# Attention scores of 32 sequences: four groups of 32 rows instead of two of 64, and the keys' two parts written from PSUM by two engines

## The reference

```python
x = x + L0_xattn(_layernorm(x), ctx, ...)      # 16 heads of 16, softmax(Q K^T * 0.25) V
x = x + L0_ffn(_layernorm(x), ...)             # one of 8 experts for each token, by argmax
x = x + L1_xattn(_layernorm(x), ctx, ...)      # 8 heads of 32, / 16, then q + attn, layer norms, Wo, relu
x = x + L1_ffn(_layernorm(x), ...)             # two of 8 experts for each token
```

## Time and profile before

| | |
|---|---|
| median of 3 runs | 2231.89 us (2225.58 to 2285.02) |
| the profiled execution's own time | 2223.33 us |
| its span | 2221.6 us |
| mean granted clock of TensorE | 0.933 |
| busy: PE, PEld | 1721.6 us (77%), 1272.6 us (57%) |
| busy: DVE, ACT, POOL | 1030.7 us (46%), 896.1 us (40%), 1033.6 us (47%) |

### The profile page before, as it was taken

How to read it: one execution, slowest core, us unless ns; L and a number is a source line. 1 busy time by engine, 2 the same in 40 slices (tenths; PEclk the granted TensorE clock), 3 DMA queues, 4 the chain that set the end, 5 groups by cost and what they waited for, 6 DMA issues and landing times. The chain is left out here.

```text
span 2221.6 us, 45766 instructions
## 1 busy us (share of the span) xinstructions
PE 1721.6 (77%) x14350; PEld 1272.6 (57%) x14351; DVE 1030.7 (46%) x2291; ACT 896.1 (40%) x1823; POOL 1033.6 (47%) x1421
## 2 busy tenths in 40 slices
PE   5888888888864999958777777777775268888884
PEld 4666666666643666646666565656664135555552
DVE  3555555555534222224555555554455724444442
ACT  3666666666641222225444444444442011111110
POOL 4656666666631111134544555454543036666663
PEclk8999999999986999978989999999997589999998
DMA  4111111000014111120111111100000222222223
GB/s 111 41 46 59 44 63 44 26 26 19 20 31 163 33 33 33 33 73 12 51 40 61 47 48 41 48 23 27 25 23 12 94 80 36 38 38 38 38 38 81
DMA packets 54163, 102.08 MB, mean 46 GB/s; under 512 B 11842, under 2 KB 37674, under 8 KB 50698
## 3 DMA queue, kind: packets, MB, share of 16 engines
q1 hardware_dynamic: 37754, 78.87, 11.0%
q0 software_dynamic: 16352, 22.47, 5.5%
HBM read 79.78 MB, written 24.93 MB: 47 GB/s over the span
## 5 line engine op out<-in xcount | busy, mean ns | idle before, releaser
L950 DVE TENSOR_REDUCE a_mx<-a_SM 100x2 bf16<-100x722 f32 x384 | 350.2, 912 | 351.1 <-PE a_SM L423 349.2
L1533 PE MATMUL e_PH<-w,e_xT 128*128 x712 | 326.5, 602 | 6.0 <-DVE e_ab L1665 2.9
L695 ACT ACTIVATE a_Pr<-a_ST 120x800 f32<-120x800 f32 (+1 forms) x288 | 241.8, 854 | 46.6 <-PE a_ST L459 46.4
L423 PE MATMUL a_SM<-a_KTb,a_QMb 64*100 64x361 bf16 x768 | 136.9, 353 | 133.2 <-DVE a_mx L950 131.0
L745 POOL TENSOR_TENSOR a_rstd<-a_ve,a_powers 100x1 f32<-100x1 f32 x192 | 117.4, 611 | 223.2 <-DVE a_ve L919 223.1
L1533 PEld LDWEIGHTS e_PH<-w,e_xT 128*128 128x128 f32 x712 | 134.8, 193 | 141.4 <-issue 138.6
L1454 POOL COPY e_gidx<-toks 128x1 int32 (+1 forms) x89 | 48.6, 546 | 300.2 <-PE e_PX L1522 206.7
L470 PE MATMUL a_M<-a_Pr,a_V 120*32 120x100 f32 (+3 forms) x4608 | 186.6, 262 | 0.3 <-ACT a_Pr L695 0.3
L423 PEld LDWEIGHTS a_SM<-a_KTb,a_QMb 64*100 64x100 bf16 x768 | 47.0, 119 | 225.8 <-DVE a_mx L950 187.1
L1619 ACT ACTIVATE e_hT<-e_PT 128x512 f32<-128x512 f32 x57 | 34.0, 597 | 332.7 <-PE e_PY L1556 309.2
L452 PE MATMUL a_ST<-a_MXM,a_ones_bf 64*120 64x400 bf16 (+1 forms) x576 | 104.1, 357 | 68.3 <-POOL a_MXM L833 67.1
(11 more groups left out here) (194 smaller groups left out, 4038.2 us busy)
## 6 DMA issues: line engine op xcount, KB each, us to landing
w<-in_E_w SPq DMA_DIRECT2D x24, 1024.0 KB, 5.9
a_ct<-in_ctx SPq DMA_DIRECT2D x64, 362.0 KB, 3.2
keep_rows<-a_keep SPq DMA_DIRECT2D x64, 100.0 KB
tile_rows<-e_y SPq DMA_DIRECT2D x32, 128.0 KB
b_rows<-in_E_b SPq DMA_DIRECT2D x1, 4096.0 KB
sums<-X SPq DMA_DIRECT2D x1, 3200.0 KB
out<-sums SPq DMA_DIRECT2D x2, 1600.0 KB, 9.4
X<-in_x SPq DMA_DIRECT2D x1, 2800.0 KB
```

What stands on the lines that cost most here:

```text
L423: last = nc.tensor.matmul(SM[0:LQ, half, 0:LK], QMb[rows, chunk, m, :], KTb[rows, chunk, :], start=True, stop=True)
L695: nc.scalar.activation(dst.rearrange("p (j q) -> p j q", j=2), ST[0:n, (b.p * NS + s) % 2, :, 0:4 * LQ], ACT.Exp, scale=SCALE).then_inc(ex ...
L950: V_.tensor_reduce(pair, SM[0:LQ, :, 0:LK], AX_X, ALU.max).then_inc(max_done, 1)
L1533: last = nc.tensor.matmul(PH[:, h, :], xT[:, c, :], rhs, start=(c == 0), stop=(c == DC - 1))
```

## The change

A product of the scores now takes 32 partitions, four groups side by side, and each group writes to a PSUM bank of its own: ST is one tile of four banks, all heads of one key tile, where it was two tiles of two. So there are 3 score blocks in both layers, each of 4 bf16 and 24 F32R products (of 200 columns in layer 0, of 100 in layer 1), and one exp of 1600 elements for each. `HT` becomes 2 and 1; layer 1 has no mask any more, `MXM` is `mxT` itself, `QM` is written by ACT and `QL` is `qf` - `QM`. `values` goes by key tile over all heads, between the score blocks. `score_rows` reads `QM` and `KT` in place of the bf16 copies, which are gone. ACT writes `KT` from PSUM (`copy_k`), DVE writes `KL` from PSUM (`low_keys`), and the latter now frees M1. `front` comes ahead of `max_columns`; `front_end` is part of `project`. In layer 1 the token-wise q is a transpose of `qf`, which holds the bias, so `bqb` is gone; on DVE `tail1a` and `tail1c` stand ahead of the maxima, on POOL `power(2, ...)` moves to the next step.

```diff
-TILE_ROWS = (64, 64)
+ROWS = 32
+GROUPS = 128 // ROWS
...
     HT = ROWS // HD
+    PER = DC * HT
...
+    NS = 3
...
-        e, j, t = pos // 8, pos % 8 // 4, pos % 4
-        if ROWS == 128:
-            return slice(0, 128), j, t
-        return slice(64 * j, 64 * j + 64), t // HT if layer == 1 else e, t % HT
+        r, t = pos // PER, pos % PER
+        return slice(ROWS * r, ROWS * r + ROWS), t // HT, t % HT
...
-        QMb = sb("QMb", [128, DC, HT, LQ], BF16)
-        KF = sb("KF", [128, DC, LK])
-        KT = [sb(f"KT{p}", [128, DC, LK], F32R) for p in range(2)]
-        KL = [sb(f"KL{p}", [128, DC, LK], F32R) for p in range(2)]
-        KTb = sb("KTb", [128, DC, LK], BF16)
+        KT = [sb(f"KT{p}", [128, DC, LKP], F32R) for p in range(2)]
+        KL = [sb(f"KL{p}", [128, DC, LKP], F32R) for p in range(2)]
...
-        MXM = sb("MXM", [128, DC, HT, LQ], BF16)
+        MXM = sb("MXM", [128, DC, HT, LQ], BF16) if layer == 0 else mxT[:].unsqueeze(2)
...
-        ST = ctx.enter_context(nc.psum_tensor(tag + "ST", [128, 2, 2, 512], F32))
+        ST = ctx.enter_context(nc.psum_tensor(tag + "ST", [128, GROUPS, 512], F32))
...
+            def project(b):
...
-            def front_end(b):
                 pe.wait_ge(qf_ready, b.count(1, 1))
                 last = project_v(b, 0, M0, 0)
                 if layer == 1:
                     for c in range(DC):
-                        last = nc.tensor.matmul(M0[0:LQ, D:2 * D], xT[:, c, :], wq[:, c, :],
-                                                start=(c == 0), stop=(c == DC - 1))
+                        last = nc.tensor.transpose(M0[0:LQ, D + c * 128:D + (c + 1) * 128], qf[:, c, :], ident[:])
...
                 if j == 0:
-                    pe.wait_ge(ktb_ready, b.count(2, 2))
-                    pe.wait_ge(qmb_ready, b.count(1, 1))
+                    pe.wait_ge(kt_ready, b.count(2, 2))
+                    pe.wait_ge(qm_ready, b.count(1, 1))
                 pe.wait_ge(max_done, b.count(NP, j))
                 for half in range(2):
-                    rows, chunk, m = place(j // 4 * 8 + half * 4 + j % 4)
-                    last = nc.tensor.matmul(SM[0:LQ, half, 0:LK], QMb[rows, chunk, m, :], KTb[rows, chunk, :],
+                    rows, chunk, m = place(half * NP + j)
+                    last = nc.tensor.matmul(SM[0:LQ, half, 0:LKP], QM[b.p][rows, chunk, m, :], KT[b.p][rows, chunk, :],
...
-                kt, eight = SLOTS[s]
-                k0, n = KTILES[kt]
-                buf = (b.p * NS + s) % 2
-                if kt == 0:
-                    pe.wait_ge(mxm_ready, b.count(EIGHTS, eight + 1))
-                    pe.wait_ge(ql_ready, b.count(EIGHTS, eight + 1))
+                k0, n = KTILES[s]
                 if s == 0:
-                    pe.wait_ge(kl_ready, b.count(1, 1))
+                    pe.wait_ge(mxm_ready, b.count(1, 1))
+                    pe.wait_ge(ql_ready, b.count(1, 1))
+                    pe.wait_ge(k_evac, b.count(2, 2))
                     if b.low >= 1:
                         pe.wait_ge(norm_read, b.count(1))
-                if b.low >= 1 or s >= 2:
-                    pe.wait_ge(exp_done, b.count(NS, s - 1))
-                C = DC // EIGHTS
-                for j in range(2):
-                    rows = place(8 * eight + 4 * j)[0]
-                    nc.tensor.matmul(ST[0:n, buf, j, 0:4 * LQ], ones_bf[rows, 0:n],
-                                     MXM[rows, C * eight:C * eight + C, :, :], start=True, stop=False)
+                if b.low >= 1 or s >= 1:
+                    pe.wait_ge(exp_done, b.count(NS, s))
+                for r in range(GROUPS):
+                    rows = place(PER * r)[0]
+                    nc.tensor.matmul(ST[0:n, r, 0:PER * LQ], ones_bf[rows, 0:n], MXM[rows, :, :, :],
+                                     start=True, stop=False)
 
                 for k, (K, Q) in enumerate(((KT[b.p], QM[b.p]), (KT[b.p], QL), (KL[b.p], QM[b.p]))):
-                    for t in range(0, 4, HT):
-                        for j in range(2):
-                            rows, chunk, _ = place(8 * eight + 4 * j + t)
-                            last = nc.tensor.matmul(ST[0:n, buf, j, t * LQ:(t + HT) * LQ], K[rows, chunk, k0:k0 + n],
-                                                    Q[rows, chunk, :, :], start=False, stop=(k == 2 and t + HT == 4))
+                    for t in range(0, PER, HT):
+                        for r in range(GROUPS):
+                            rows, chunk, _ = place(PER * r + t)
+                            last = nc.tensor.matmul(ST[0:n, r, t * LQ:(t + HT) * LQ], K[rows, chunk, k0:k0 + n],
+                                                    Q[rows, chunk, :, :], start=False, stop=(k == 2 and t + HT == PER))
                 last.then_inc(st_ps, 1)
 
-            def values(b, g, last_exps=False):
-                for kt in range(3):
-                    n = KTILES[kt][1]
-                    if last_exps and kt == 2:
-                        pe.wait_ge(exp_done, b.count(NS, NS))
+            def values(b, kt):
+                n = KTILES[kt][1]
+                pe.wait_ge(exp_done, b.count(NS, kt + 1))
+                for g in range(NG):
                     for j in range(HG):
                         h = g * HG + j
                         last = nc.tensor.matmul(M0[VW * j:VW * (j + 1), g * LQ:(g + 1) * LQ],
                                                 V[b.p][0:n, kt, h, :], Pr[0:n, kt, POS[h] * LQ:(POS[h] + 1) * LQ],
-                                                start=(kt == 0), stop=(kt == 2))
+                                                start=(kt == 0 and g == 0), stop=(kt == 2 and g == NG - 1))
...
             def step(b, fr, ahead, back, tail):
                 nxt, nxt2, prev = b.plus(1), b.plus(2), b.plus(-1)
+
+                def rows_of(*pairs):
+                    if fr:
+                        for j in pairs:
+                            score_rows(nxt, j)
+
+                if fr:
+                    front(nxt)
                 if back:
                     max_columns(b)
                 if fr:
-                    front(nxt)
+                    project(nxt)
                 if back:
                     scores(b, 0)
-                if fr:
-                    front_end(nxt)
-                pair = 0
-                for s in range(NS):
-                    if back:
-                        if s == 4:
-                            pe.wait_ge(exp_done, b.count(NS, 3))
-                            free_m0(nxt, fr)
-                            values(b, 0)
-                        if s > 0:
-                            scores(b, s)
+                rows_of(*((0, 1), (0,))[layer])
+                if back:
+                    scores(b, 1)
+                if tail:
                     if fr:
-                        score_rows(nxt, pair)
-                        pair += 1
-                    if tail and s == 2 + (1 - layer):
-                        if fr:
-                            pe.wait_ge(v_evac, nxt.count(2, 1))
-                        out_transposes(prev, layer == 1, prev.low >= LAG)
-                for g in range(EARLY, NG):
-                    if back:
-                        late = g == max(EARLY, EARLY_EXPS)
-                        if late:
-                            pe.wait_ge(exp_done, b.count(NS, NS - 1))
-                        if g == 0:
-                            free_m0(nxt, fr)
-                        last = values(b, g, late)
-                    if tail and g == 1:
-                        out_product(prev, layer == 1, prev.low >= LAG)
-                    if fr and layer == 0 and g == 2:
-                        score_rows(nxt, 6)
+                        pe.wait_ge(v_evac, nxt.count(2, 1))
+                    out_transposes(prev, layer == 1, prev.low >= LAG)
+                rows_of(*((2,), (1,))[layer])
                 if back:
-                    last.then_inc(av_ps, 1)
+                    free_m0(nxt, fr)
+                    values(b, 0)
+                rows_of(*((3,), ())[layer])
+                if back:
+                    scores(b, 2)
+                rows_of(*((), (2,))[layer])
+                if back:
+                    values(b, 1)
+                rows_of(*((4,), ())[layer])
+                if tail:
+                    out_product(prev, layer == 1, prev.low >= LAG)
+                rows_of(*((5,), ())[layer])
+                if back:
+                    values(b, 2).then_inc(av_ps, 1)
+                rows_of(*((6,), ())[layer])
                 if ahead:
                     start_k(nxt, nxt2, prev, tail)
-                if fr:
-                    score_rows(nxt, NP - 1)
+                rows_of(NP - 1)
...
             def copy_k(b, h):
 
-                act.wait_ge(kl_ready, b.count(1))
-                act.wait_ge(ktb_ready, b.count(2))
                 act.wait_ge(k_ps, b.count(2, h + 1))
```

(89 more changed lines are left out.)

99 lines of the change are left out of this document (35 added, 64 removed).

## The result

The changed kernel takes 2174.12 us (median of 4, 2173.72 to 2176.48) against 2258.0 us (median of 4, 2225.58 to 2285.02). The ratio is 0.9757, 95% interval 0.9731 to 0.9784; it is that of the undisturbed executions, hence nearer to 1 than the two medians. Run again (e12) the kernel had 0.9695, 0.9655 to 0.9736. So it is faster by 2.4 to 3%, where I had forecast 2140 us, 4.1% under the median of 2232 that I had. The profiled execution took 2174.32 us, 49.0 less than the one before; I had laid out 92.

A forecast was written before the change was run, and what follows sets the result against it. Layer 0 was taken as mostly TensorE's own work, layer 1 as a ring of waits. 2223.3 - 10 (layer 0) - 82 (layer 1) = 2131 us profiled, median 2140; own range 2095 to 2185, 8 in 10 from 2080 to 2235.

The forecast's parts named there:

- the last one of layer 1: Layer 1's TensorE waits: longest hole shrinks to 1.7 us, so the low clock, 0.68 us of the mean step, goes.
- Rival 3: Clock in both layers: each pays 0.68 us a step, + 42 us, median 2182; chance 0.12.
- Layer 1's step: Layer 1's attention stage: a step goes from 22.15 to 19.5 us, 82 us over 31 intervals.
- S0 to S1: Layer 1's first to second score block: starts at 7.0 and 9.85 us, the second waiting for the first exp.
- S1 to S2: Layer 1's second to third score block: starts at 9.85 and 12.8 us, with value products between.
- The POOL wait: Layer 1, before the scores: TensorE's 2.3 us wait for POOL's masked maximum goes.
- TensorE's wait for DVE ahead of the value products: Layer 1: q done at 2.75 us, the second `low_keys` ends at 4.4, value products start at 4.45.
- Layer 0's step: Layer 0's attention stage: a step goes from 19.34 to 19.0 us, 10 us over 31 intervals.
- the seven spacings of rows: Layer 0's eight row products: seven spacings of 1.36 us, bounded by DVE, 9.5 us whatever TensorE does.
- Rivals 1, 2 and 5: Four-group score rounds: two at a time, median 2239, chance 0.12; hindering each other, from 2278, 0.06; short rounds cheaper, 2103, 0.1.
- rival 5: Score rounds on TensorE: 100 columns cost 0.05 us, 200 cost 0.09; median 2103 us; chance 0.1.
- Rival 4: DVE becomes the ring, `low_keys` holding M1: 1.4 us more a step, + 87 us, median 2227; chance 0.1.

The follow-up runs named there:

- e12: The changed kernel, unedited, run once more against the kernel before: 2159.33 us.
- e1: The changed kernel with unread 128-row products put into TensorE's waits in both layers, against the kernel before: 2088.63 us, ratio 0.9367.
- e11: e1 run once more, against the kernel before: 2093.07 us, ratio 0.9399.
- e2: The changed kernel with the filling of e1 over 32 rows only, against the kernel before: 2120.44 us, ratio 0.9499.
- e5: The changed kernel with the filling of e1 over 64 rows, against the kernel before: 2112.67 us, ratio 0.9431.
- e9: The changed kernel with only the 8 filling products of e1 ahead of layer 1's value products, against the kernel before: 2132.91 us, ratio 0.96.
- e6: e1 with layer 1's second `low_keys` ahead of `tail1b` and 2 instead of 8 fillers before its value products, against the kernel before: 2139.15 us, ratio 0.9569.
- e4: The changed kernel with two groups of 64 rows in layer 0 alone, against the kernel before: 2199.35 us, ratio 0.9879.

## Why the prediction was wrong

The time lay inside the stated range and the direction was right, but the gain forecast, 92 us, came as 49. The step that failed is the last one of layer 1: "TensorE's longest hole, 2.25 us or more before, is then 1.7, so I take the low clock away as well".

- **The clock.** The longest hole did shrink, and the clock went down to 0.83 in place of up to 1.00. Layer 1 runs at 17.9 us a step at full clock, the mean of the loop's two steps, and took 20.64: 2.75 x 31 = 85 us. Layer 0 runs at 18.75 and took 19.16: 13 us. Rival 3 had the place right and the size wrong, 42 us for both, since it took the price of the kernel before. e1 and e11 show that the loss is the clock: the same kernel with its waits filled gets 86 and 66 us back. The change halves the score products' columns and rows and shortens the holes; I counted only the holes. What makes the clock fall is not settled: e2 and e5 rule out idle time alone, e9 the longest hole alone, and e6 beside e9 speaks against the plain sum of filling. Whether the fewer rows or the fewer columns of the score products lowered the clock was not tested apart. The Trainium skill, TensorE: Matmul & The Clock Gate, section Why this matters for your kernels, keeps the clock up by leaving no long idle gaps between bursts. That is not enough in this trace: behind layer 1's first step no wait of TensorE was over 1.75 us, it was busy for 554 of 640 us (83% of the two full-clock steps), and the clock was 0.83, while before it had waits of 2.25 us in every step, was busy 73% of the time, and had 0.94.
- **Layer 1's step** was laid out as 19.5 and is 17.9 at full clock: 50 us too slow. S0 to S1 is 1.84 us (1435.81 to 1437.65) where I had 2.85. Of that 1.0, 0.7 is the exp, laid out with 1600 elements and 1.55 us where layer 1 has 800 and 0.84; the other 0.3 is the block itself and its drain, laid out too long. S1 to S2 is 2.50 (1437.65 to 1440.15, right behind the value products) where I had 2.95. The POOL wait went as forecast; TensorE's wait for DVE ahead of the value products came where it was forecast, 1.16 us in this step and up to 1.73 in others, for 1.7 laid out.
- **Layer 0's step**, 19.0, is 18.75 (21 of its 31 steps ran at full clock, 18.7 to 18.9): 8 us too slow. The mechanism is half right. Of the seven spacings of rows one is 1.34 and four are 1.42 to 1.52, near the 1.36 that DVE's maximum sets, but two are 2.00 and 1.94, those with a score block between. With blocks 0.64 us longer (e4) the step grew by 1.65, so TensorE's own work bounds a part of it.
- **Together** 2131 - 50 - 8 + 85 + 13 + 3 = 2174. Two errors of opposite sign met, which is luck: with layer 1's and layer 0's steps laid out right, the clock would have been the whole miss, about 100 us. The median of 2140 has 8.6 us more, the distance of the earlier profiled execution from its median; the changed kernel's median and profiled execution lie 0.2 us apart.
- **Rivals 1, 2 and 5** are out: rounds take 0.105 us with four groups, for 200 and for 100 columns. The Trainium skill's rule beside rival 5 (TensorEngine Tiling (Array Packing), Theoretical Speedup) gives 64 rows up to two times and 32 up to four times the throughput, so at most 2 from one to the other: a block of layer 0 shrank by 1.76 (1.48 to 0.84, e4), near that rule, one of layer 1 from 0.93 at most (1312.54 to the value product at 1313.47) to 0.73 us, a factor of 1.3, far from it. That the load of 120 weights sets the short round fits both, but no run changed it alone.
- **Rival 4** is half there: `low_keys` holds TensorE in both layers, but at no more than its laid out price.

## What to carry to other kernels

Where a change takes work from TensorE or gives each of its products fewer rows, read the granted clock of that stage as a term of the sum, not only its waits: here it ate 98 us (85 + 13) of the 150 that the full-clock steps promise (0.6 and 4.25 us, x 31). A clock that was lost here could be bought back with products that nobody reads, placed in waits on a bank that is free there; how many rows they had counted, and the number of them alone did not tell what they would give. And a step that alternates between clocks has to be compared at its full-clock steps, and, in a loop of two, with its own counterpart, before its waits are argued over. Last, redo the element counts for every layer that a change touches: here an exp of 1600 elements was carried over to a layer that has 800, and the forecast was 0.7 us a step out by it.

## What the runs showed that was not expected

- Filling TensorE's waits with unread products shortened the kernel by 86 us (2174 to 2089; 66 us, 2159 to 2093, the second time), with 980 more products in the two stages (14 a step in layer 0, 18 in layer 1).
- Layer 1's clock was 0.98 filled with 128 rows, 0.95 with 64, 0.93 with 32, though TensorE idled for 22, 13 and 18 us there; unfilled it was 0.83, with 86 us idle.
- Six filling products fewer a step together with a shorter wait (e6 against e1) cost 50 us, though the real work was the same.
- Four row groups with weights of their own run beside each other at 0.105 us a round, as two groups did.
